# Attention with unsplit float32 probabilities: the values as stationary operand on four 32-column strips

## The reference

```python
q = (query @ Wq.T + bq)   # 16 heads of 16 channels
k = (key @ Wk.T + bk)
v = (value @ Wv.T + bv)
scores = jnp.einsum('bhsd,bhtd->bhst', q, k) / math.sqrt(D)
attn = jax.nn.softmax(scores, axis=-1)
out = jnp.einsum('bhst,bhtd->bhsd', attn, v)
out = out.transpose(0, 2, 1, 3).reshape(B, S, E)
return out @ Wo.T + bo
```

## Time and profile before

| | us |
|---|---|
| median of 3 runs | 1118.36 |
| lowest and highest of them | 1117.96, 1123.08 |
| the profiled execution | 1119.13 |
| its span from first to last instruction | 1117.3 |

### The profile page before, as it was taken

The page is one execution under the profiler, slowest core; times in us unless marked ns, Lnnn a source line. Parts: engine busy times, 40 slices in busy tenths (PEclk is TensorE's granted clock), DMA queues, the critical chain, the costliest instruction groups (busy, mean ns, idle before and its releaser), DMA issues.

```text
span 1117.3 us, 20415 instructions
## 1 busy us (share of the span) xinstructions
PE 952.8 (85%) x6981; PEld 825.7 (74%) x6981; DVE 776.6 (70%) x1538; ACT 581.0 (52%) x1112; POOL 436.6 (39%) x479
## 2 busy tenths in 40 slices
PE   2798878748987999999837888885989999999995
PEld 2577667536877999999825767665678888888885
DVE  5688787866664777777655687795686666667665
ACT  5375675745234667667546877874622232322221
POOL 1465556240663666666415444334012212212210
PEclk9989999859998999999956899996899999999999
DMA  3300750010325888888540000001000001000002
GB/s 129 110 21 1 189 144 1 1 61 1 128 82 193 237 231 233 227 221 233 119 134 1 20 20 1 1 2 43 15 15 29 28 14 28 17 26 28 14 0 76
DMA packets 44281, 85.81 MB, mean 77 GB/s; under 512 B 4161, under 2 KB 31041, under 8 KB 44097
## 3 DMA queue, kind: packets, MB, share of 16 engines
q0 software_dynamic: 14784, 46.44, 15.1%
q1 hardware_dynamic: 29440, 38.61, 11.9%
HBM read 64.25 MB, written 20.79 MB: 76 GB/s over the span
## 4 chain that ended last, share of the span: by engine, by line
PE 48%; DVE 20%; ACT 11%; issue 9%; DMA 7%; POOL 4%; DVEq 0%; ACTq 0%; POOLq 0%
PE bank L1179 31%; PE bank L1215 8%; DMA w_raw<-in_fw,w_idx 4%; DVE nmax L1034 3%; PE bank L1274 3%; DVE probT_lo L1063 2%; PE bank L1364 2%; DVE prob L1037 2%; POOL sorted_x L375 2%; ACT xn L512 2%; DMA summed<-y_sb,tile_to 2%; ACT probT_hi L654 1%; ACT o_raw L644 1%; PE bank L1343 1%; ACT w_hi L533 1%
## 5 line engine op out<-in xcount | busy, mean ns | idle before, releaser
L1179 PE MATMUL bank<-xT_hi,w_hi 128*128 128x512 f32 x352 | 139.9, 398 | 2.2 <-DVE hid L964 2.2
L581 ACT ACTIVATE act_sb<-bank 128x512 f32<-128x512 f32 x88 | 52.6, 598 | 167.8 <-PE bank L1179 167.7
L1179 PE MATMUL bank<-xT_lo,w_hi 128*128 128x512 f32 x352 | 139.3, 396 | 0.0
L1179 PE MATMUL bank<-xT_hi,w_lo 128*128 128x512 f32 x352 | 139.1, 395 | 0.0
L964 DVE TENSOR_TENSOR hid<-bank,act_sb 128x512 f32<-128x512 f32 x88 | 60.8, 691 | 107.3 <-ACT act_sb L581 107.1
L332 POOL TENSOR_TENSOR w_hi<-w_raw,zero_col 128x768 fp32r<-128x768 f32 (+1 forms) x20 | 31.9, 1595 | 262.9 <-PE bank L1215 236.8
L951 DVE SCALAR_TENSOR_TENSOR xres<-bank,gate,xres 128x256 f32<-128x256 f32 x320 | 132.6, 476 | 0.8 <-PE bank L1215 0.8
L1364 PE MATMUL bank<-ident,prob 128*128 128x128 f32 x512 | 86.2, 298 | 31.9 <-DVE probT_lo L1063 26.0
L1063 DVE TENSOR_TENSOR probT_lo<-bank,probT_hi 128x512 f16<-128x512 f32 x128 | 88.0, 687 | 32.4 <-ACT probT_hi L654 31.8
L1179 PE MATMUL bank<-xsT_hi,w_hi 128*128 128x256 f32 x368 | 106.5, 289 | 2.3 <-DVE xsT_lo L918 1.5
L1215 PE MATMUL bank<-w_hi,hid_hi 128*128 128x256 f32 x352 | 99.5, 283 | 6.2 <-DVE hid_lo L972 6.2
(11 more groups left out here) (199 smaller groups left out, 2763.5 us busy)
## 6 DMA issues: line engine op xcount, KB each, us to landing
w_raw<-in_fw SPq DMA_DIRECT2D x18, 384.0 KB, 3.0
sorted_x<-empty_row SPq DMA_DIRECT2D x2, 2967.0 KB, 21.4
xs<-sorted_x SPq DMA_DIRECT2D x23, 258.0 KB, 3.4
ctx_raw<-in_ctxT SPq DMA_DIRECT2D x8, 512.0 KB, 5.2
aw_raw<-in_aw SPq DMA_DIRECT2D x10, 256.0 KB, 3.8
summed<-empty_row SPq DMA_DIRECT2D x1, 2304.0 KB, 29.6
xres<-in_x SPq DMA_DIRECT2D x4, 512.0 KB, 5.7
xn_all<-summed SPq DMA_DIRECT2D x4, 512.0 KB, 5.9
```

The source lines that it names most:

```text
L581: nc.scalar.activation(act_sb[:, (ls * J + j) % 2, :], bank[2 * ((ls * J + j) % 2) + 1][:], ACT.Silu).then_inc(f["act"], 1)
L1179: last = nc.tensor.matmul(dst, lh, rh, start=(i == 0), stop=(i == len(pairs) - 1))
```

## The change

The turned probabilities stay float32 and in one piece (`probT`). `weighed` now takes the values as the stationary operand: 16 columns of value, one column of ones and 15 of zeros, 32 float32 columns a head (`v_full`, `VW` is 32). The 128 float32 columns of the turned probabilities move. Head h of a group writes partitions 32h to 32h+31 of bank 6 or 7, one 32-column strip of the array per head. The four groups of a sequence fill the bank. A float32 matmul of this kind stands as two instructions in a trace, as those of L1343 do now. The outputs lie transposed, so ACT copies the bank (`o_turned`) and PE turns it back by four transposes into the same bank (`turned_back`, in steps 7, 11 and 15 and behind the next block's values). DVE then takes the reciprocals and makes two multiplications straight out of PSUM (`outputs`). `probT_lo`, the parts of the values and POOL's work on the outputs are gone. The values are stored by four DVE additions instead of two. The first `weighed` of a block waits for the addition of the block before.

```diff
-                        dve.wait_ge(a["phi"], n * GROUPS + (i + 1))
-                        nc.vector.tensor_tensor(probT_lo[:, i % RINGT, :], bank[4 + i % 2][:],
-                                                probT_hi[:, i % RINGT, :], ALU.subtract).then_inc(a["plo"], 1)
-                        if i >= 5 and i % 2 == 1:
-                            denominators(n, (i - 5) // 2)
+                        if i >= 8 and i % NG == 0:
+                            outputs(n, i // NG - 2)
...
+                def outputs(n, b):
+                    dve.wait_ge(a["oback"], n * BLK + b + 1)
+                    back = bank[6 + b % 2][:].rearrange("p (h w) -> p h w", w=VW)
+                    nc.vector.reciprocal(rden[:, b % 2, :], back[:, :, HD]).then_inc(a["rden"], 1)
+                    dve.wait_ge(a["rden"], n * BLK + b + 1)
+                    for u in range(2):
+                        nc.vector.tensor_tensor(
+                            o_sb[:, b, 8 * u:8 * u + 8].rearrange("p (g j) d -> p g j d", g=NG),
...
-                nc.gpsimd.memset(v_parts[:, :, :, HD:HD + 2], 1.0).then_inc(a["vones"], 1)
+                nc.gpsimd.memset(v_full[:], 0.0).then_inc(a["vset"], 1)
+                pool.wait_ge(a["vset"], 1)
+                nc.gpsimd.memset(v_full[:, :, :, HD], 1.0).then_inc(a["vset"], 1)
...
-                        if i >= 4 and i % 2 == 0:
-                            output_copy(n, i // 2 - 2)
-                    output_copy(n, 6)
-                    output_copy(n, 7)
-                    if build:
-                        values_high(n + 1)
+                        if i >= 6 and i % NG == 2:
+                            output_copy(n, i // NG - 1)
+                    output_copy(n, BLK - 1)
...
                 def weighed(n, i):
 
                     b, g = divmod(i, NG)
-                    pe.wait_ge(a["plo"], n * GROUPS + (i + 1))
-                    if i == 0:
-                        pe.wait_ge(a["vlo"], n * 2 + 2)
-                    if b >= 1 and g % 2 == 0:
-                        pe.wait_ge(a["ocopy"], n * 8 + (2 * b - 2 + g // 2 + 1))
+                    pe.wait_ge(a["pcopy"], n * GROUPS + (i + 1))
+                    if i == 0 and n > 0:
+                        pe.wait_ge(a["xadd"], n * 2)
+                    if b >= 2 and g == 0:
+                        pe.wait_ge(a["o"], 2 * (n * BLK + b - 1))
                     for h in range(GRP):
-                        u, j = divmod(h, 2)
-                        head = 8 * u + 2 * g + j
-                        at_col = VW * (4 * u + 2 * (g % 2) + j)
-                        for part, p in enumerate((probT_hi, probT_lo)):
-                            last = nc.tensor.matmul(bank[6 + g // 2][:, at_col:at_col + VW],
-                                                    p[:, i % RINGT, S * h:S * (h + 1)],
-                                                    v_parts[:, b, head, :], start=(part == 0), stop=(part == 1))
+                        last = nc.tensor.matmul(bank[6 + b % 2][32 * h:32 * h + VW, S * g:S * (g + 1)],
+                                                v_full[:, b, 8 * (h // 2) + 2 * g + h % 2, :], probT[:, i % RINGT, S * h:S * (h + 1)],
+                                                start=True, stop=True)
                     last.then_inc(a["pv"], 1)
+
+                def turned_back(n, b):
+
+                    pe.wait_ge(a["ocopy"], n * BLK + b + 1)
+                    for g in range(NG):
+                        last = nc.tensor.transpose(bank[6 + b % 2][:, S * g:S * (g + 1)],
+                                                   o_turned[:, b % 2, S * g:S * (g + 1)], ident[:])
+                    last.then_inc(a["oback"], 1)
...
                         if i >= 2:
                             weighed(n, i - 2)
+                        if i >= 7 and i % NG == 3:
+                            turned_back(n, i // NG - 1)
                     weighed(n, GROUPS - 2)
                     weighed(n, GROUPS - 1)
                     if build:
                         values(n + 1)
-
-                    pe.wait_ge(a["plo"], n * GROUPS + GROUPS)
-                    pe.wait_ge(a["o"], n * 8 + 8)
+                    turned_back(n, BLK - 1)
+
+                    pe.wait_ge(a["o"], 2 * (n * BLK + BLK))
```

109 lines of the change are left out of this document (33 added, 76 removed).

## The result

The changed kernel takes 1138.93 us in the median of four runs (1136.24 to 1142.1), the kernel before 1119.69 in the median of four runs beside them (1117.96 to 1123.08). The ratio is 1.0167, with a 95% interval of 1.0133 to 1.0201: **slower by 1.7%**. The profiled execution took 1138.74 us, with a span of 1137.0.

The account below looks back on a forecast made before the run. DVE and ACT were taken to bound steps 0 to 11 through a ring, PE the build. Terms +13.5 - 6.4 - 2.4 + 1 = +5.7 on 1119.1 gave 1124.8, less 0.8 to the median: 1124.0 us, range 1108 to 1147.

Parts of the forecast that it names:

- the partial overlap of the strips: Rival for `weighed`: column strips overlap only in part, four heads take five passes, `weighed` 0.77 us, total 1142; chance 0.15.
- The other signs: Four `weighed` instructions starting within 0.03 us, PE gap about 1 us before output transposes, these 7 to 8 after last-block step 12.
- three blocks of layer 0, without the clock: Building blocks of layer 0, each +0.5 us in steps 0 to 11, +0.5 in the build, +1.3 at the end.
- three blocks of layer 1, without the clock: Building blocks of layer 1, each +0.9 us in steps 0 to 11, 0.0 in the build, +1.3 at the end.
- last blocks up to the output transposes: Last block of each layer: -1.35 and -0.9 us in steps 0 to 11, -2.1 twice from step 12; together -6.4.
- clock behind them: After denser last-block work, half of the 4.8 us that both layers could get back from the low clock: -2.4.
- clock in the building blocks: First steps of each layer: PE runs at 1.2 GHz, so each added `weighed` costs double, +1 us.
- the ring of the kernel before: Steps 0 to 11: a dependency loop through DVE and ACT, from subtraction to next subtraction, sets 3.66 us per two steps.
- The price of `weighed`: On PE, one new `weighed` takes 0.45 us (0.40 to 0.50), 0.25 more than now; four transposes take 0.46.
- Both strip rivals: Column strips in `weighed` overlap only in part (1142 us, chance 0.15) or not at all (1177 us, chance 0.08).
- The wait in steps 7 and 11: PE waits for ACT's output copy before `turned_back`: 1.7 us as laid out, 1 to 2 us as a sign.
- The end of a block: From the values to next step 0: PE idle 1.7 us, DVE's `oT_lo` 1.3 us later; +1.3 us in both layers.

Follow-up runs that it names:

- dense matmuls ahead: The changed kernel plus unused 128x512 matmuls behind the first scores, 28 in layer 0 and 12 in layer 1: 1119.11 us, ratio 1.0013 to the kernel before.
- one dense matmul a step: The changed kernel plus one unused 128x512 matmul in each of steps 0 to 11 of each layer's first block: 1124.64 us, one run, beside 1118.72.
- transposes twice: The changed kernel with every probability transpose in steps 0 to 11 of each layer's first block made twice: 1125.69 us, one run, beside 1123.28.
- POOL waits: The changed kernel with POOL's output-bias additions to x in layer 0 held until DVE's two constants are done: 1134.5 us, ratio 1.0138 to the kernel before.
- the kernel before with dense matmuls: The kernel before plus the same unused matmuls behind the first scores of each layer: 1116.9 us, ratio 0.9985 to the kernel before.

## Why the prediction came out as it did

The measured 1138.93 lies in the range (1108 to 1147), and 1.7% slower is on the side that had the largest chance. The forecast of 1124.0 is 15 us too low. It is not the partial overlap of the strips, whose 1142 lies nearer, that happened. That the time lies in the range is luck: its upper part was there for that rival, and the clock filled it. By its own signs the forecast was wrong: two of the three blocks of layer 0, with 57.7 and 50.8 us, do not lie within 1 us of 48.3, nor does an undisturbed one with 47.1, and the wait of PE in step 11 was 0.77 and not 1 to 2. The other signs came as written, save that PE's next work follows 0.36 behind the first `weighed` row and not 0.4 to 0.5. By its terms:

| term | forecast | measured |
|---|---|---|
| three blocks of layer 0, without the clock | 3 x 2.3 | 3 x 1.1 |
| three blocks of layer 1, without the clock | 3 x 2.2 | 3 x 1.1 |
| last blocks up to the output transposes | -6.4 | -3.6, -2.7 |
| clock behind them | -2.4 | -2.0, -2.1 |
| prologue of layer 0 | 0 | +3.8 |
| clock in the building blocks | +1 | +9.9, +1.4, +3.7, +5.0 |

The blocks "without the clock" are the undisturbed ones: 47.1 us in layer 0 (second block with dense matmuls ahead; 47.1 also with one a step), 42.2 in layer 1. The last line is what the first three blocks of layer 0 and the first of layer 1 took beyond +1.1 on the kernel before, whose own first blocks hold 4 us of low clock.

**The clock was the step that failed.** "In the first steps of each layer, PE runs at 1.2 GHz and each added `weighed` costs double: +1." This takes the length of the half-clock stretch as given. It grew instead, and in it PE becomes the bound: two steps take 5.3 us (67.66 to 72.93), where the ring of the kernel before had 3.66 at the full clock. Timeline of PE at the half clock:

```profile
67.66 2.08 PE L1297 MATMUL bank<-k_half,q_full 32*128 32x256 f32 x8
69.67 1.12 PE L1318 MATMUL bank<-ident,prob 128*128 128x128 f32 x4
70.71 0.66 PE L1331 MATMUL bank<-probT,v_full 128*32 128x128 f32 x8
71.30 1.12 PE L1318 MATMUL bank<-ident,prob 128*128 128x128 f32 x4
72.35 0.66 PE L1331 MATMUL bank<-probT,v_full 128*32 128x128 f32 x8
72.93 0.80 PE L1297 MATMUL bank<-k_half,q_full 32*128 32x256 f32 x2
```

Scores 2.0, four transposes 1.04, a `weighed` 0.59, where the full clock gives 1.06, 0.59 and 0.36. The first block then cost 9.9 and 5.0 us instead of 1. The removal of the low clock (dense matmuls ahead) returned 11.2 and 7.8. That the low clock cost this is shown; why the new form kept it longer is not. The falls of the clock in the second and third blocks of layer 0 (131.6 to 135.0 and 179.4 to 189.6) cost 1.4 and 3.7 us. Two kernels with the same steps there have none (one dense matmul a step, transposes twice), two have one (POOL waits, dense matmuls ahead), and the kernel before with dense matmuls has one as well. So they vary by execution, and that the change makes them is not shown.

**POOL beside DVE was missed.** The prediction counted POOL's lost work as harmless: "DVE and POOL lose work and may run more freely". What stood behind that work on POOL moved up, beside two DVE instructions on the path: +3.0 us. The kernel in which POOL waits showed it. The other 0.8 us of the prologue is clock again: in this execution it was at the half from 42.9 to 46.3 us, with projections that start 0.43 apart instead of 0.23. Four other kernels of the new form lack that fall and start the mask at 48.7 to 49.0 us, as the kernel before does (48.87). The Trainium skill (GPSIMD Engine Reference, section 1, Specifications) lists the SBUF interfaces as shared with VectorE. The traces agree: 3.33 against 1.24 us for the same instruction, and 2.30 against 0.15 for the next, with and without L325 beside them.

**The price of `weighed` was right**, and it was the main unknown. Forecast: 0.46 + 0.45 = 0.91 a step with the transposes. Measured 0.95, and 0.23 for one in a row. My 0.40 to 0.50 put both changes of the array's division on the `weighed`, which takes 0.36; 0.13 shows on the transposes ahead of it. Both strip rivals are out. The Trainium skill (TensorE: Matmul & The Clock Gate, Part 3, The mechanism) says that weight loads overlap running matmuls only if their row groups differ. All four strips read the same 128 rows, their loads start within 0.05 us while matmuls run, and eight loads with their passes took 0.23 us, so it does not hold for column strips here. Its 2.38 times for three column tiles pointed the right way.

**The wait in steps 7 and 11** came where it was laid out, and smaller: 1.43 us in step 7 of layer 0 (forecast 1.7), 0.77 in step 11 and in both steps of layer 1. So steps 0 to 11 cost +0.2 in layer 0 instead of +0.5 and +0.4 in layer 1 instead of +0.9.

**The end of a block** was over-sized. From the first unit to the next step 0 the kernel took +0.9 in layer 0, not +1.8, and +0.7 in layer 1, not +1.3. The gap before the output transposes is there (0.87 of PE idle, 1.47 with the transposes back). The step that fell is that "`oT_lo` comes 1.3 us later". The storing additions lie beside 1.1 us of output transposes. From the start of these to the projection it was 2.66 us (111.28 to 113.94), where the kernel before took 3.25 (95.89 to 99.14).

**The last blocks**: 7.2 us from step 12 to the output transposes (forecast 7.4), steps 0 to 11 in 18.9 and 19.6 (18.85 and 19.05). The clock held through the projection, and from the output transposes on the two layers gave back 4.1 us where I had taken half of 4.8, a figure that the prediction gives without its working.

So with the clock of the building blocks and the prologue set aside the forecast was too high: 1119.1 + 6.6 - 6.3 - 4.1 gives 1115.3, just faster than before. What turned this into a loss was mainly the longer low clock in the first blocks.

## What to carry to other kernels

Where a trace shows the half clock in a stretch, ask what the change does to the length of that stretch, not only what each added instruction costs in it; price both with a few unused matmuls put ahead of it. A change that takes work from an engine off the path also moves up what is queued behind that work: look which instruction on the path it will run beside. Taking matmul work away at the half clock can cost time, and adding some can gain it; here single executions say so for work in the steps, and ten runs for work ahead of them.

## What was not expected of the hardware

- PE can be busy in all of 30 us, by the record, and stay at a granted clock of 0.50 (1.2 GHz). With 28 unused matmuls of 512 columns before it (6.8 us), and 12 in layer 1, the clock stayed at 1.00 in both first blocks, and the kernel was 20 us faster.
- With the transposes of twelve steps doubled, the first block of layer 0 was 5.8 us shorter than in the kernel after and the one of layer 1 no longer (one run): the clock came back sooner.
- Four 32-column strips over the same 128 rows, in float32: eight passes of 128 columns in 0.23 us in a row, 0.36 with a switch from whole-array transposes.
- Beside POOL additions of 128 x 1024 in SBUF, a DVE instruction of 1.24 us took 3.33 and one of 0.15 took 2.30. In nine traces, of the larger one and POOL's first addition, whichever started first kept its time, and the other took 1.0 to 2.1 us longer.
